# Conditional residual kernel: adapters in falling order, first chunks loaded ahead of the ids, and a last slot in three parts

## What is computed

```python
itok_B_0_15 = jax.random.randint(..., (128,), 0, 16, jnp.int32)
itok_B_3_7 = jax.random.randint(..., (128,), 3, 8, jnp.int32)
...
W = L0_cond_weights[itok_B_0_15]                 # (128, 64, 64)
x = x + jnp.einsum('bct,bcd->bdt', x, W)
w = L1_cond_weight[itok_B_3_7]                   # (128, 1024, 1024)
x = x + jnp.einsum('bsi,boi->bso', x, w)
```

## Time and profile before

| | us |
|---|---|
| median of 3 runs | 796.64 (796.27 to 796.71) |
| the profiled execution | 796.8 |
| its span | 795.1 |
| TensorE busy | 778.8 (98%) |
| VectorE busy | 590.6 (74%) |
| ScalarE busy | 457.1 (57%) |
| POOL busy | 254.5 (32%) |

### The profile page before, as it was taken

One profiled execution on the slowest core, in us unless ns is written; L12 is line 12 of the kernel. 1 busy time (PEld: TensorE's weight loads), 2 busy tenths in 40 slices (PEclk: granted clock), 3 DMA queues, 4 the chain that ended last, 5 costly groups with the idle time before them and its releaser, 6 DMA issues.

```text
span 795.1 us, 19206 instructions
## 1 busy us (share of the span) xinstructions
PE 778.8 (98%) x3448; PEld 645.2 (81%) x3449; DVE 590.6 (74%) x706; ACT 457.1 (57%) x772; POOL 254.5 (32%) x158
## 2 busy tenths in 40 slices
PE   5999999999999999999999999999999999999996
PEld 5788888888888888888888888888888888888885
DVE  7688887788887567888876788887576756756765
ACT  3465566557656555665655566556554654654554
POOL 2444533253452212435421243452122122122110
PEclk9999999999999999999999999999999999999999
DMA  8334443444442333454333444432332233233233
GB/s 264 96 108 147 144 141 107 137 130 126 148 120 65 106 100 119 122 146 145 96 102 106 123 125 136 155 101 86 106 98 77 75 106 90 68 106 99 62 104 80
DMA packets 73955, 90.89 MB, mean 114 GB/s; under 512 B 13781, under 2 KB 64470, under 8 KB 73942
## 3 DMA queue, kind: packets, MB, share of 16 engines
q1 hardware_dynamic: 63574, 57.97, 24.0%
q10 hardware_dynamic: 10368, 32.78, 14.3%
HBM read 57.15 MB, written 33.55 MB: 114 GB/s over the span
## 4 chain that ended last, share of the span: by engine, by line
PE 96%; DMA 1%; DVE 1%; issue 0%; POOL 0%; ACT 0%; ACTq 0%; SPq 0%; DVEq 0%; POOLq 0%
PE z_ps L544 15%; PE z_ps L545 15%; PE first_ps L544 15%; PE first_ps L545 15%; PE z_ps L547 15%; PE first_ps L547 13%; PE y_ps L557 7%; DMA w_nat<-in_L_cond_weight_dram 1%; DVE y L927 0%; PE y_ps L525 0%; PE first_ps L525 0%; DVE z_parts L920 0%; ACT y L669 0%; POOL w_nat L315 0%; ACTq L215 0%
## 5 line engine op out<-in xcount | busy, mean ns | idle before, releaser
L356 POOL TENSOR_TENSOR xt_lo<-x_turned,xt_hi 128x1024 fp32r<-128x1024 f32 x61 | 146.7, 2405 | 249.9 <-ACT xt_hi L653 248.4
L544 PE MATMUL z_ps<-w_hi,xt_hi 128*128 (+1 forms) x528 | 205.8, 390 | 0.0
L544 PE MATMUL first_ps<-w_hi,xt_hi 128*128 x528 | 205.5, 389 | 0.0
L545 PE MATMUL z_ps<-w_lo,xt_hi 128*128 (+1 forms) x528 | 205.4, 389 | 0.0
L545 PE MATMUL first_ps<-w_lo,xt_hi 128*128 x528 | 205.4, 389 | 0.0
L927 DVE TENSOR_TENSOR y<-y_ps,y 64x512 f32<-64x512 f32 x254 | 174.6, 689 | 33.6 <-ACT y L669 27.7
L547 PE MATMUL z_ps<-w_hi,xt_lo 128*128 (+1 forms) x512 | 199.2, 389 | 0.0
L547 PE MATMUL first_ps<-w_hi,xt_lo 128*128 x480 | 186.7, 389 | 0.0
L669 ACT ACTIVATE y<-y_ps 64x512 f32<-64x512 f32 x254 | 150.5, 594 | 11.3 <-issue 2.2
L658 ACT ACTIVATE z_parts<-z_ps 64x512 fp32r<-64x512 f32 x132 | 78.5, 595 | 132.6 <-PE y_ps L557 93.4
L658 ACT ACTIVATE z_parts<-first_ps 64x512 fp32r<-64x512 f32 x132 | 78.5, 595 | 131.4 <-PE y_ps L557 103.6
(11 more groups left out here) (135 smaller groups left out, 360.0 us busy)
## 6 DMA issues: line engine op xcount, KB each, us to landing
x_in<-in_x_dram SPq DMA_DIRECT2D x536, 64.0 KB, 2.4
out_dram<-y ACTq DMA_DIRECT2D x124, 256.0 KB, 3.6
w_nat<-in_L_cond_weight_dram SPq DMA_DIRECT2D x128, 128.0 KB
w_nat<-in_L_cond_weight_dram SPq DMA_DIRECT2D x4, 512.0 KB, 6.6
y<-in_L_cond_weight_dram SPq DMA_DIRECT2D x2, 512.0 KB, 7.1
w_turned<-in_L_cond_weights_dram SPq DMA_DIRECT2D x2, 256.0 KB, 3.8
x_in<-in_x_dram SPq DMA_DIRECT2D x2, 256.0 KB, 4.6
x_turned<-in_L_cond_weight_dram SPq DMA_DIRECT2D x1, 512.0 KB, 5.3
```

What stands on the lines that cost most here:

```text
L356: nc.gpsimd.tensor_tensor(xt_lo[h][:], x_turned[h][:], xt_hi[h][:].bitcast(F32), ALU.subtract).then_inc(xt_lo_made, 1)
L544: nc.tensor.matmul(to, xt_hi[h][:, t, :], whi, start=(t == 0), stop=False)
L545: mm = nc.tensor.matmul(to, xt_hi[h][:, t, :], wlo, start=False, stop=last and not pair)
```

## The change

- **Order of adapters.** Ids are replaced by 7 - id for sorting and turned back where an address is needed, so adapters come in falling order, 7 first.
- **Loads.** Right after the ids' row, before anything is known, SP loads chunks 0 to 4 of adapter 7 (the last). If the first adapter turns out to be another, the five are loaded a second time; else their semaphores are raised. x of slot 0, chunks 5 to 7 and then w0 follow.
- **Ids.** The condition ids come as a row too; both are clipped as rows and spread over the partitions by two matmuls into `ids_ps`. Eight turns of the identity run before (`WARMING`).
- **Turns.** `TURN_ORDER` puts x of slot 0 after chunk 4; four turns stand before the gathering matmuls; the last turn, of chunk 7, stands inside z of slot 0, after three tiles; the first half of z waits for six of the nine turns.
- **VectorE.** The lo of the first chunks are put between the small operations of the table's chains; `keep_x0_lo` looks at `first_samples_i` instead of the table and comes before the table is done.
- **The end.** The last slot's z is made in three parts (512, 256 and 256 columns) and its y straight on the right partitions by two matmuls of 64 rows, so that one copy takes the place of across and add. SP stores sample a and the first half of b, ScalarE the second half of b.

```diff
-        TURN_ORDER = [0, 1, X0, 2, 3, 4, 5, 6, 7]
-        FOR_FIRST_HALF = 5
+        AHEAD_OF_IDS = 5
+        TURN_ORDER = [0, 1, 2, 3, 4, X0, 5, 6, 7]
+        FOR_FIRST_HALF = 6
+        WARMING = 8
+        LAST_TURNS = 1
+        TILES_FIRST = 3
...
+        last_z_banks = [z_banks[1][0], z_banks[1][1], z_banks[1][0]]
+        LAST_COLUMNS = [slice(0, HALF), slice(HALF, HALF + HALF // 2), slice(HALF + HALF // 2, T)]
...
             pool.wait_ge(w0_hi_made, 1)
+            pool.wait_ge(table_ready, 1)
...
+            for c in range(AHEAD_OF_IDS):
+                sp.dma_start(first_nat[c], adapter_rows[((NAD - 1) * CHUNKS_PER_GROUP + c) * P:((NAD - 1) * CHUNKS_PER_GROUP + c + 1) * P, :]).then_inc(first_loaded[c], 16)
...
+            with sp.If(first_ad < NAD - 1):
+                for c in range(AHEAD_OF_IDS):
+                    sp.wait_ge(first_loaded[c], 16)
+                    load_first(c)
+            with sp.Else():
+                for c in range(AHEAD_OF_IDS):
+                    sp.sem_inc(first_loaded[c], 16)
+            sp.wait_ge(samples_made, 2)
...
+            for c in range(AHEAD_OF_IDS, CHUNKS_PER_GROUP):
+                if c >= OWN_PLACE:
+                    sp.wait_ge(first_turned, NH * TURN_OF[c - OWN_PLACE] + NH)
+                load_first(c)
             with nc.allow_non_contiguous_dma(reason="rows of one condition"):
                 for lo in (0, C):
                     sp.dma_start(w0_nat[lo:lo + C], cond_rows).then_inc(w0_loaded, 16)
...
+            for _ in range(WARMING):
+                nc.tensor.transpose(first_banks[2][0][:, 0:P], ident[:], ident[:])
+            pe.wait_ge(row_clipped, 1)
+            nc.tensor.matmul(ids_ps[:, 0:1], clipped_row, ones[0:1, 0:1], start=True, stop=True)
+            pe.wait_ge(row_clipped, 2)
+            nc.tensor.matmul(ids_ps[:, 1:2], cond_row, ones[0:1, 0:1], start=True, stop=True).then_inc(ids_spread, 1)
...
-            turn_first(0)
+            for i in range(TURNS + 1):
+                turn_first(i)
             pe.wait_ge(hot_made, 1)
...
-            for i in range(1, len(TURN_ORDER)):
+            for i in range(TURNS + 1, len(TURN_ORDER) - LAST_TURNS):
                 turn_first(i)
-            pe.wait_ge(table_made, 1)
+            pe.wait_ge(samples_made, 2)
             stores = look_first_stores(pe)
             def first_half(pair):
                 pe.wait_ge(first_lo_made, NH * FOR_FIRST_HALF)
-                sum_z(0, 0, 0, pair)
+                sum_z(0, 0, 0, pair, range(0, TILES_FIRST))
+                for i in range(len(TURN_ORDER) - LAST_TURNS, len(TURN_ORDER)):
+                    turn_first(i)
+                sum_z(0, 0, 0, pair, range(TILES_FIRST, KT))
...
             def last_half(pair):
-                sum_z(1, 1, buf, pair, range(0, KT // 2))
-                sum_y(s, pair, last_y_banks, (0,))
-                sum_z(1, 1, buf, pair, range(KT // 2, KT))
+                sum_last_z(1, pair)
+                sum_last_y(0, pair)
+                sum_last_z(2, pair, range(0, KT - 1))
                 pe.wait_ge(y_made, PER_Y * (2 * pairs_past) + (PER_Y + MADE_AHEAD))
-                sum_y(s, pair, last_y_banks, (1,))
+                sum_last_y(1, pair)
+                sum_last_z(2, pair, range(KT - 1, KT))
+                sum_last_y(2, pair)
...
+            act.wait_ge(y_summed, PER_Y * before + 2)
+            keep_z_hi(s, 1, 0)
+            act.wait_ge(y_stored[0], 32 * pairs_past + STORED_AHEAD)
             act.wait_ge(y_stored[1], 32 * pairs_past + STORED_AHEAD)
+            act.wait_ge(y_summed, PER_Y * before + 4)
+            place_w0(s)
...
+            begin_half_y(0)
+            keep_last_z_hi(1)
+            begin_half_y(1)
+            take_last_y(0)
+            take_last_y(1)
+            keep_last_z_hi(2)
+            take_last_y(2)
...
+            keep_z_lo(s, 1, 0)
+            finish_half_y(0)
+            keep_last_z_lo(1)
+            finish_half_y(1)
+            take_last_y(0)
+            take_last_y(1)
+            keep_last_z_lo(2)
+            take_last_y(2)
```

More of the change, by code:

```diff
@@ L319, in _ @@
                 add_1_to_first(c)
-            for c in range(4, 6):
+            for c in range(4, CHUNKS_PER_GROUP):
                 add_1_to_first(c)
@@ new lines, in _, with keep_last_z_hi @@
+            _, sample, stores = look(act, s, SAMPLE_A, STORES)
+            stores_before, = look(act, before, STORES)
+            act.wait_ge(y_summed, PER_Y * before + 2)
+            keep_z_hi(s, 1, 0)
+            act.wait_ge(y_stored[0], 32 * pairs_past + STORED_AHEAD)
+            act.wait_ge(y_stored[1], 32 * pairs_past + STORED_AHEAD)
+            act.wait_ge(y_summed, PER_Y * before + 4)
+            place_w0(s)
+            def keep_last_z_hi(part):
+                act.wait_ge(z_summed, NH * s + part + 1)
+                for k in range(2):
+                    nc.scalar.activation(z_parts[rows_of(k), 1, k, LAST_IN_HALF[part]],
+                                         last_z_banks[part][rows_of(k), LAST_IN_BANK[part]], ACT.Copy).then_inc(z_hi_made, 1)
@@ L730, in _, with begin_half_y @@
+            def begin_half_y(n):
+                with act.If(stores_before > 1):
+                    across(before, 0, n, True)
+                with act.Else():
+                    across(before, 0, n, False)
+            begin_half_y(0)
[5 more added lines that the diff above has]
+            take_last_y(2)
             with act.If(stores > 1):
-                last_half(True)
+                act.wait_ge(last_made[1], LAST_PARTS)
+                act.dma_start(out_rows[bass.ds(sample * C, C), HALF:T], y[1][rows_of(1), HALF:T]).then_inc(last_stored, 16)
@@ L747, in _, with step, stepped, keep_first_lo @@
             dve.sem_inc(y_made, MADE_AHEAD)
-            def keep_first_lo(i):
+            def step(ins):
+                chain[0] += 1
+                ins.then_inc(dve_step, 1)
+            def stepped():
+                dve.wait_ge(dve_step, chain[0])
+            def keep_first_lo(i, halves=range(NH)):
                 what = TURN_ORDER[i]
-                for n in range(NH):
+                for n in halves:
                     at = (slice(None), 0, slice(n * TPB, (n + 1) * TPB), slice(what * P, (what + 1) * P))
@@ new lines, in _ @@
+            nc.vector.tensor_copy(vals[:, 0:1], row[:])
+            nc.vector.tensor_copy(vals[:, 1:2], ids[:, 1:2])
+            nc.vector.tensor_copy(vals[:, 2:4], own[:, 1:3])
+            nc.vector.memset(vals[:, 4:5], 1.0)
+            stepped()
+            nc.vector.tensor_scalar(hot[0], col2, pos[:, 0:1], None, ALU.is_equal)
+            nc.vector.tensor_scalar(hot[1], col2, 1.0, pos[:, 0:1], ALU.add, ALU.is_equal).then_inc(hot_made, 1)
+            keep_first_lo(2, (1,))
+            keep_first_lo(3)
@@ new lines, in _ @@
+            keep_first_lo(4, (1,))
+            keep_x0_lo(TURN_OF[X0])
+            stepped()
+            step(nc.vector.tensor_scalar(fill[:], got[:, 0, 0:2], absent[:, 0:1], None, ALU.mult))
+            link(nc.vector.tensor_scalar(rank[:, 1:2], rank[:, 0:1], float(CHUNKS_PER_GROUP), None, ALU.min))
+            step(nc.vector.scalar_tensor_tensor(out=rank[:, 2:3], in0=got[:, 0, 3:4], scalar=float(CHUNKS_PER_GROUP),
+                                                in1=rank[:, 1:2], op0=ALU.mult, op1=ALU.add))
```

349 lines of the change are left out of this document (194 added, 155 removed).

## The result

The changed kernel takes 802.67 us (median of 6 runs, 802.16 to 803.70), the kernel before 796.67 in the same runs: ratio 1.0071, 95% interval 1.0060 to 1.0081. It is slower, by 0.6 to 0.8%, and lies in the predicted range, 1.7 us above the predicted 801.0.

A forecast was written before the change was run, and what follows sets the result against it. TensorE was taken to bound the kernel (96% of the span), so only the two ends could matter: 796.8 + 4.1 (start) + 0.5 (end) = 801.4, less 0.2 for the median and 0.2 for the table, 801.0 us; range 797.6 to 804.0.

The forecast's parts named there:

- Counts at 7.7, `hot` at 13.9, z from about 19.5: Start: counts read at 7.7, not 7.24; hot at 13.9, not 10.82; z from about 19.5, some 4.2 us earlier.
- The table 5.25 us later, at 20.7: Start: with lo halves put between its operations, the table is ready at 20.7 instead of 15.45.
- "2.5", "2.5" and "some 0.3": Last step to the table: four lo halves 2.5 us, small operations 2.5, less some 0.3 of latency covered.
- x of slot 1 lands 8.8 us after the table; slot 1 at 35.3, a wait of 3.9: Slot 1: x lands at 29.5; TensorE begins at 35.3 after waiting 3.9 us, 0.7 later than before.
- The chunk moves by the same 5.25, +2.25 at slot 2, +4.1 at y: Next adapter's first chunk shifts with the table; TensorE at least 2.25 us later at slot 2, 4.1 at slot 1's y.
- The two deadlines: Slot 2's x lo with 3.0 us of slack, and slot 1's third y matmul with 1.15 us.
- The end +0.5, bounds -1.5 to +2.0: Kernel's end, last slot: costs 0.5 us, between 1.5 gained and 2.0 lost.
- Y of part 0 needs `w0_parts`, which ACT now copies only after it has seen the store of slot 63 land, ... so at about 7.0: End: y of the last slot's first part can go about 7.0 us after the hi of slot 64.
- last add 11.2: End: TensorE, at 9.6, must wait for VectorE's last add of slot 64, 11.2 us after slot 64's hi.
- The last quarter pays: End, lower bound: all adds hidden and the shorter last quarter paid in full give -1.5 us.
- The rival had it fall and stay low through slot 1: Rival, slot 1: TensorE's clock stays low for all 11.8 us of work, 5.9 lost, 803.5 us; chance 0.12.
- The two rivals that won time: Chunk's landing does not move with its issue, 797.8, chance 0.11; end gives more than start takes, 793.5, chance 0.09.

The follow-up runs named there:

- f2: Changed kernel with the table ahead of VectorE's last lo halves and x of slot 2 issued by ACT instead of SP: 798.62 us, ratio 1.0025.
- f0: Control: changed kernel with two slot fields held at zero or more by one maximum in a register: 802.51 us, ratio 1.0078.
- g3: Changed kernel with ACT's wait for the store moved and its two slot-field loads done before its loop: 799.79 us.
- f1: Changed kernel with ACT's wait for the store moved and its two slot-field loads put behind the last slot's w0: 800.38 us.
- g1: Changed kernel with the start of f2 and the end of g3: 796.30 us, ratio 0.9986 to the kernel before.
- e1: Changed kernel, bounds stated, with ACT waiting for the last store only where it overwrites y[1], and VectorE waiting for it too: 802.87 us.
- e0: Control: changed kernel with two slot fields read with a stated bound: 803.86 us, ratio 1.0086.
- e2: Changed kernel, bounds stated, with VectorE's lo of chunk 4 and slot 0's x put behind the table's last operation: 802.96 us.
- f6: Changed kernel without the eight warming turns (WARMING = 0): 802.99 us.
- g2: Changed kernel with the start of f2 and the end of the kernel before: 796.08 us, ratio 0.9990 to the kernel before.

## Why the prediction was right, and where it was not

It was right in sign and range, and in the chain of the start. Both of its terms were off, one up, one down; against the profiled execution it summed to 801.4 and the profile had 803.7: the start was 1.7 too dear, the end 3.9 too cheap. That the sum came within 1.7 us is therefore part luck: with the start as forecast, the end's error alone would have given 804.9, outside the range. The start's mechanism was foreseen; of the end's, the store and the adds were, and the loads, its largest part, were not.

- *Counts at 7.7, `hot` at 13.9, z from about 19.5.* Measured 7.42, 13.34 to 13.61, and 18.62. The counts came 0.2 later than before, where 0.45 was taken.
- *The table 5.25 us later, at 20.7.* It came 4.1 later, at 19.56. Up to the gathered rows at 15.5 the sum was 0.3 too high. From there the terms as written, "2.5", "2.5" and "some 0.3", give 20.5 and not 20.7, so 0.2 is a slip of the sum; what follows took 4.0 us, where they add to 4.7. The step that failed is this last one: the halves covered more of the latency of the small operations than the 0.3 allowed.
- *x of slot 1 lands 8.8 us after the table; slot 1 at 35.3, a wait of 3.9.* Landed 8.3 after it; slot 1 at 33.80, a wait of 3.1. Right, with the table's error in it. It was 0.8 earlier than before, not 0.7 later.
- *The chunk moves by the same 5.25, +2.25 at slot 2, +4.1 at y.* The issue moved by 3.1 (1.0 of the table's shift was won back in SP's 16 issues, 9.0 us instead of 10.0), the add by 3.8; PE was 1.0 late at slot 2, 1.8 at the third y and 2.3 at the fourth, which the forecast had no wait for (54.98, where 52.64 was its time), so 2.4 at the mark. The two deadlines and their order were right, and f2 shows that the chain is the one named: take the chunk and the table 5.5 and 2.6 us forward, and the mark moves by 3.3.
- *The end +0.5, bounds -1.5 to +2.0.* Measured +4.4 in the profile, +3.9 in f0, outside the bounds. The step that failed is "Y of part 0 needs `w0_parts`, which ACT now copies only after it has seen the store of slot 63 land, ... so at about 7.0": it came at 9.0 after the mark. The store was named; it landed 5.5 us after its issue began. What was not in the sum are the two loads into registers ahead of the hi, some 2 us with nothing to hide them, and the one more that `place_w0` makes after the store has landed (0.49 of the 0.86 us between 789.53 and 790.39). g3 moves the two loads and the store's wait and gets 2.7 back. The step after it ("last add 11.2") was right as to what is late next: PE did wait for those adds, 2.9 us in f1.
- *The last quarter pays.* It doesn't. With both obstacles gone (g3, g1) the new end takes 17.5 to 17.6 from the mark and the old one 16.8 to 17.0; the chain hi, w0, copy, add of slot 64 sets the end, and a shorter last part leaves it as it is.
- *The clock.* The rival had it fall and stay low through slot 1 at 0.12. It fell in 6 of the 8 profiles with the wait of 2.9 to 3.4 us there (not in the changed kernel's own and not in f1), and in none of the four with 0.8 to 1.2. So it was likelier than its chance, and cheaper than its price: it was back 3 to 7 us after it fell, and what PE lost it saved in the waits behind. The windows of f0:

```profile
34.00:36.00 2.00, 1.80 (x7) 1.50 (x8) 1.97 (x2) 0.76 (x2) 0.00 (x0) 0.87 0.00 0
36.00:38.00 2.00, 2.00 (x7) 1.52 (x6) 0.94 (x2) 0.63 (x1) 0.00 (x0) 0.50 0.29 90
38.00:40.00 2.00, 2.00 (x8) 1.61 (x7) 0.00 (x0) 0.00 (x0) 0.00 (x0) 0.77 0.27 92
```

f0 has the low clock and no wait at slot 2 or at y, the changed kernel the high one and both waits. Their marks are 0.7 us apart, f0's the earlier, but their first chunks landed at different times too. Two pairs differ up to their marks in little but the clock. The first chunk in f0 (low), then in f1 (high):

```profile
43.14 0.46 POOL L312 TENSOR_TENSOR w_nat<-w_nat,ident 128x128 f32 x1 [9.25 <-DMA w_nat<-in_L_cond_weight_dram]
43.00 0.46 POOL L312 TENSOR_TENSOR w_nat<-w_nat,ident 128x128 f32 x1 [9.34 <-DMA w_nat<-in_L_cond_weight_dram]
```

Their marks are 780.69 and 780.49. In e1 (low) and the changed kernel (high) the chunk is there at 44.24 and 44.26, the marks are 781.65 and 781.40. So the low clock in slot 1 cost some 0.4 us at most (e1 also began slot 1 0.15 sooner), where the prediction left 0.6 of 4 unhidden, and between the pairs a chunk 1.1 to 1.3 us later moved the mark by about 0.9: the chunk's landing sets it. The prediction's "1.2 and then 2.4 GHz" at the start is read from the durations of the turns; the granted clock in the earlier trace rows is 1.00. The Trainium skill, "TensorE: Matmul & The Clock Gate" (Part 1, the HAM clock gate), has an idle TensorE fall to half rate and return after sustained work. Six of the eight profiles agree with the fall, and all six with the return.
- *The two rivals that won time* fell: the chunk did move with its issue, and the end gave nothing.

What stays open: why the first chunk lands 8.5 us after its issue in f0 and f1, and 10 in the changed kernel; what the loads would give if moved alone; and how much of the 0.7 us between the changed kernel's 20.6 and e0's 19.9 at the end is the low clock, which e0 did not have there. Where it stayed low for some 7 us (the changed kernel, e2) the end took 20.5 to 20.6, where for some 3 (f0, f2, f6) 19.8 to 20.2. A run that keeps PE busy through that wait was not made.

## What to carry to other kernels

When a change makes one engine's first work earlier by moving small control operations behind it, price the queue that waits for those operations (here the table, then SP's loads in order) before the gain: slot 0 began 5.1 us sooner and slot 1 only 0.8. Behind a loop, look at what each engine's queue does before its first instruction there; a register load that is free while the engine works costs 0.3 to 1.3 us when it stands idle. The timeline does not name it: there, look for an idle time laid to "issue", or to a releaser that the code does not wait for, and then ask for the chain that ended last, which has it as ACTq with the helper's line. And when a wait is removed, read the one behind it first: the store, the loads and the adds lay one over another, and the store's wait of 3.1 us was worth 1.0 when it was moved alone.

## What the runs showed of the hardware

- Two loads of table fields into ACT's registers, with the engine idle, took about 2 us: the hi came 2.69 (f2) to 3.08 us (e2) after the y matmuls began, and 0.84 (g3) to 0.96 us (g2) after them without the loads ahead of it. In e1's chain they are 1.31 and 0.28 us, 1.8 with what lies between.
- A store of 512 KB in two DMAs, issued from 784.07 on, landed at 789.53 (4.82 us after 784.71, in the chain of waits), and ACT, which waited for it, loaded two more fields (0.49 us) and went on at 790.39.
- After about 3 us without work the clock's level was not the same from run to run. In the end's wait, of 3.0 to 3.4 us, the changed kernel, e2, f0, f2 and f6 fell to 1.2 GHz, and e0, with 3.1 us, stayed at 2.4. The windows of the changed kernel, whose 256-column matmuls went out every 0.21 us in place of 0.12:

```profile
789.00:790.00 1.00, 0.00 (x0) 0.00 (x0) 0.57 (x1) 0.00 (x0) 0.00 (x0) 0.99 0.00 0
790.00:791.00 1.00, 0.17 (x1) 0.18 (x2) 0.00 (x0) 0.47 (x2) 0.00 (x0) 0.50 0.00 0
792.00:794.00 2.00, 2.00 (x9) 1.74 (x8) 1.89 (x4) 1.90 (x5) 0.00 (x0) 0.50 0.00 0
```
